# The gate's tanh in its PSUM bank, and the gate's place in the order of a tick

## What is computed

```
logits = x2 @ gate_w.T; the 2 best of 8 experts get softmax weights, the others 0
for each expert e (and the shared one, weight 1):
    a = x2 @ w1[e] + b1[e];  b = x2 @ w3[e] + b3[e]
    y += weight[e] * ((silu(a) * b) @ w2[e] + b2[e])
out = layernorm(x2 + y)
```

## Time and profile before

| | |
|---|---|
| median of 3 runs | 1234.33 us |
| lowest, highest | 1233.46, 1239.96 us |
| span of the profiled execution | 1224.7 us (its own time beside the span isn't shown) |
| TensorE busy | 929.7 us, 76% |
| VectorE busy | 922.6 us, 75% |
| GpSimd busy | 528.2 us, 43% |
| ScalarE busy | 489.6 us, 40% |
| mean granted TensorE clock | 0.798 of full |

### The profile page before, as it was taken

How to read it: one execution, slowest core, us unless ns; L and a number is a source line. 1 busy time by engine, 2 the same in 40 slices (tenths; PEclk the granted TensorE clock), 3 DMA queues, 4 the chain that set the end, 5 groups by cost and what they waited for, 6 DMA issues and landing times.

```text
span 1224.7 us, 13783 instructions
## 1 busy us (share of the span) xinstructions
PE 929.7 (76%) x3960; PEld 700.9 (57%) x3960; DVE 922.6 (75%) x1323; ACT 489.6 (40%) x911; POOL 528.2 (43%) x311
## 2 busy tenths in 40 slices
PE   4845549668689899577689899486789896677996
PEld 2434435256468685165477785165468683554885
DVE  2699996589999966689999965789789965322233
ACT  3534423544246434454345424454245421211442
POOL 1266540453457740533367730544257741001553
PEclk9855558778669999678679899678579997665999
DMA  5100101201023211101023211201023212000331
GB/s 193 36 35 35 52 1 35 70 35 61 18 70 121 77 45 54 70 35 61 18 78 127 73 36 55 85 18 61 18 72 119 86 35 91 21 1 9 117 109 42
DMA packets 38254, 72.61 MB, mean 59 GB/s; under 512 B 3871, under 2 KB 12712, under 8 KB 38174
## 3 DMA queue, kind: packets, MB, share of 16 engines
q1 hardware_dynamic: 38174, 71.65, 17.8%
HBM read 65.14 MB, written 2.30 MB: 55 GB/s over the span
## 4 chain that ended last, share of the span: by engine, by line
PE 45%; DVE 23%; issue 20%; POOL 6%; ACT 3%; DVEq 1%; POOLq 0%; DMA 0%; ACTq 0%; SPq 0%
PE ps L862 11%; DVE hs L1051 7%; PE ps L939 7%; PE ps L718 6%; PE ps L797 5%; POOL dbu L531 4%; DVE yacc L1103 4%; PE ps L836 3%; PE ps L791 2%; PE ps L825 2%; DVE work L1219 2%; PE ps L881 2%; PE ps L776 2%; DVE xn L1014 1%; POOL work L563 1%
## 5 line engine op out<-in xcount | busy, mean ns | idle before, releaser
L531 POOL TENSOR_TENSOR dbu<-v,bbc 128x1024 f32<-128x1024 f32 x128 | 308.9, 2418 | 257.3 <-DVE hs L1051 136.3
L1051 DVE TENSOR_TENSOR_SCAN hs<-ps,carry,dbu 128x512 f32<-128x512 f32 x256 | 313.3, 1266 | 10.1 <-ACT ps L627 8.2
L627 ACT ACTIVATE ps<-delta,neg_a 128x512 f32<-128x512 f32 x256 | 175.7, 692 | 300.5 <-DVE hs L1051 300.4
L718 PE MATMUL ps<-ident,hs 128*128 128x128 f32 x1024 | 189.1, 344 | 116.5 <-DVE yacc L1103 99.5
L718 PEld LDWEIGHTS ps<-ident,hs 128*128 128x128 f32 x1024 | 157.0, 180 | 150.0 <-DVE hs L1051 72.4
L1103 DVE SCALAR_TENSOR_TENSOR yacc<-ps,ctok,yacc 128x512 f32<-128x512 f32 x240 | 167.3, 737 | 1.2 <-PE ps L718 1.0
L555 POOL TENSOR_TENSOR w_lo<-w13s,w_hi 128x512 fp32r<-128x512 f32 x72 | 94.5, 1313 | 145.1 <-ACT w_hi L693 145.1
L939 PE MATMUL ps<-w2s,work 128*128 128x256 f32 x576 | 140.4, 388 | 0.3
L939 PEld LDWEIGHTS ps<-w2s,work 128*128 128x128 f32 x576 | 109.0, 196 | 15.9 <-DVE work L1225 1.5
L1219 DVE SCALAR_TENSOR_TENSOR work<-work 128x512 f32<-128x512 f32 x72 | 82.3, 1143 | 46.5 <-POOL work L563 45.6
L862 PE MATMUL ps<-x_hi,w_hi 128*128 128x512 f32 x288 | 107.9, 457 | 9.4 <-DVE work L1225 9.2
(11 more groups left out here) (159 smaller groups left out, 1243.0 us busy)
## 6 DMA issues: line engine op xcount, KB each, us to landing
w13s<-in_w SPq DMA_DIRECT2D x72, 256.0 KB, 2.9
bbc<-brow_dram SPq DMA_DIRECT2D x32, 512.0 KB, 4.0
w2s<-in_w SPq DMA_DIRECT2D x36, 256.0 KB, 2.7
cbc<-comb_dram SPq DMA_DIRECT2D x32, 256.0 KB, 3.5
work<-work SPq DMA_DIRECT2D x16, 256.0 KB, 2.3
xn<-in_x SPq DMA_DIRECT2D x5, 512.0 KB, 5.3
xt<-in_x SPq DMA_DIRECT2D x4, 512.0 KB, 3.6
rope<-in_rope_q SPq DMA_DIRECT2D x4, 512.0 KB, 4.2
```

What stands on the lines that cost most here:

```text
L531: pool.tensor_tensor(dbu[:, i % DRING, :, :], v[:, 2 * h:2 * h + 2, :], bbc[:, n // 2 % 2, n % 2, :].rearrange("p (o t) -> p o t", o=1) .t ...
L627: act.activation(ps[:, unit % 2, :], delta[:, q, :], ACT.Exp, scale=neg_a[:, q * NS + m:q * NS + m + 1]).then_inc(da_done.sem, 1)
L718: last = pe.transpose(ps[:, bank, t * P:(t + 1) * P], src(t), ident[:, :])
L1051: dve.tensor_tensor_scan(hs[:, m % 2, q, 0:TC], ps[:, unit % 2, :], dbu[:, n % DRING, q % 2, :], carry[:, m, q:q + 1], ALU.mult, ALU.add). ...
```

## The change

The tanh no longer writes `th` in SBUF but overwrites the bank from which it reads, and the product `gm` reads it there. So the bank is busy for longer: the next gate may only start when the product is done, where before it could when the tanh was. The tanh waits for `ga`, which reads the same bank. To this come moves in the order of a tick: the gate's matmuls go from the early to the late part (behind the up matmuls, the scan's transposes and, in the first ticks, the combine transposes and the bias rows, ahead of the down product); `gate_halves` goes from mid to late, behind the scan's exponentials and ahead of the copy of the combine weights; the product `gm` goes from late to mid, ahead of the scans. The exponentials `el` stay where they were. `hh`, the weight split, `gac` and the DMA issues keep their places.

```
-        th = work[:, 0:1024].rearrange("p (a t) -> p a t", a=2)
...
 ScalarE, second
                 if part == "mid":
-                    gate_halves(j, t)
+                    if t == T_TOP:
+                        act.wait_ge(*ls_done.at(j, 1))
+                        act.activation(el[:, :, :], ls[:, :, :], ACT.Exp).then_inc(el_done.sem, 1)
                     return
                 if part == "late":
+                    gate_halves(j, t)
...
             def gate_halves(j, t):
-                if t == T_TOP:
-                    act.wait_ge(*ls_done.at(j, 1))
-                    act.activation(el[:, :, :], ls[:, :, :], ACT.Exp).then_inc(el_done.sem, 1)
...
                     act.activation(ga[:, ib, :], ps[:, 4, :], ACT.Identity, scale=0.5, bias=bias
                                    ).then_inc(ga_done.sem, 1)
-                    act.activation(th[:, ib, :], ps[:, 4, :], ACT.Tanh, scale=0.5, bias=bias
+                    act.wait_ge(*ga_done.at(j, c + 1))
+                    act.activation(ps[:, 4, :], ps[:, 4, :], ACT.Tanh, scale=0.5, bias=bias
                                    ).then_inc(th_done.sem, 1)
...
 TensorE, second_early
                 c = t - T_EXP
-                if 0 <= c < 2 * ALL:
-                    e, ib = divmod(c, 2)
-                    pe.wait_ge(*lo_done.at(j, c + 1))
-                    pe.wait_ge(*th_done.at(j, c))
-                    gate_rows(j, c, 0, a_ps)
                 if 0 <= c - 1 < 2 * ALL:
                     pe.wait_ge(*hh_done.at(j, c - 1))
                     gate_rows(j, c - 1, 1, b_ps)
...
 TensorE, second_late, ahead of the down product
+                c = t - T_EXP
+                if 0 <= c < 2 * ALL:
+                    pe.wait_ge(*lo_done.at(j, c + 1))
+                    pe.wait_ge(*gm_done.at(j, c))
+                    gate_rows(j, c, 0, a_ps)
...
 VectorE: gated_rows(j, t) is called at the end of second_mid, up_rows(j, t) in second_late
+            def gated_rows(j, t):
                 c = t - T_EXP - 1
                 if 0 <= c < 2 * ALL:
                     ib = c % 2
...
-                    dve.scalar_tensor_tensor(out=gm[:, ib, :], in0=th[:, ib, :], scalar=1.0,
+                    dve.scalar_tensor_tensor(out=gm[:, ib, :], in0=ps[:, 4, :], scalar=1.0,
                                              in1=(gac if c >= 2 else ga)[:, ib, :],
                                              op0=ALU.add, op1=ALU.mult).then_inc(gm_done.sem, 1)
+
+            def up_rows(j, t):
+                c = t - T_EXP - 1
+                if 0 <= c < 2 * ALL:
+                    ib = c % 2
                     dve.wait_ge(*gm_done.at(j, c + 1))
                     dve.wait_ge(*b_ps.at(j, c + 1))
```

More of the change, by code:

```diff
@@ L1171, in second_mid @@
                                           ).then_inc(x2lo_done.sem, 1)
+                gated_rows(j, t)
             def relu_rows(j, half):
@@ L1209, in second_late @@
                     combine_weights(j)
+                up_rows(j, t)
+                if t == T_OUT:
+                    for tile in range(NT):
+                        dve.wait_ge(*o_ps.at(j, 2 * ALL))
+                        dve.tensor_tensor(xa[:, tile, :], ps[:, 6 + tile // 2, tile % 2 * DM:(tile % 2 + 1) * DM],
+                                          x2[:, tile, :], ALU.add).then_inc(xo_done.sem, 1)
+                    for tile in range(NT):
+                        row_stats(j, "xo", xa, tile, xo_done)
+                    deviations(j, "xo")
+                    normalise(j, "xo", xa, xa, fin_done)
+            def gated_rows(j, t):
                 c = t - T_EXP - 1
@@ L1226, in second_late @@
                                              in1=gm[:, ib, :], op0=ALU.add, op1=ALU.mult).then_inc(hh_done.sem, 1)
[L1227 to L1235, removed]
             def wide(a):
```

## The result

| | before | after |
|---|---|---|
| median | 1233.89 us (4 runs, 1231.65 to 1239.96) | 1373.76 us (4 runs, 1370.64 to 1380.93) |
| span of the profiled execution | 1224.7 us | 1368.7 us |
| mean granted clock | 0.798 | 0.795 |

The ratio on record is 1.1216, 95% interval 1.1156 to 1.1276. The two medians of the table give 1.113 and the two spans 1.118, so the changed kernel is 11 to 12% slower. In this and all later comparisons the ratio leaves out executions that were over 1.5% longer than the kernel's fastest, while medians and ranges keep them. The forecast was 1394 us, with 1360 to 1430 as its range.

What follows compares the result with a forecast made beforehand. Beside scans TensorE and VectorE were taken as full; the new order closes a loop over four engines. Span 1224.7 + 100.5 (three chunks) + 41.5 (last chunk) + 18 (clock) = 1384.7, plus 9.6 to the median: 1394 us, range 1360 to 1430.

Steps and rivals of the forecast that it cites:

- The loop: Beside scans: second exponential, ga, th, w_hi, w_lo, gac, gm, back to the scans; 8.54 us a tick against 6.5.
- The small steps: Links of the tick beside scans: exponential to ga 0.70, gac to gm 1.38, gm to scans 0.70 us.
- The turn after the scans: Behind the scans and in the last chunk, gm to gate and round to gm through TensorE: 7.24 us.
- Extras: Next chunk's four squares on ScalarE, 1.6 us, and four normalisations on VectorE, about 1.0 beyond its wait.
- The stretched product: VectorE's L1219, one operand now in PSUM: 1.143 to 0.75 us, 28 us less busy time over 72 instances.
- tanh in place: ScalarE's tanh writing PSUM: 0.69 us; waiting for ga, it starts 0.75 after ga's start.
- The last two ticks: End of each chunk's experts, no weights to split, ga straight to gac: 4.7 us each, 9.4 in all.
- The clock term: Gate at low clock, 1.17 us more in 31 ticks without scans: between 0 and 36 us, taken as 18.
- the step from the span to the median of the runs: Median of the runs lies 9.6 us above the profiled span, added to 1384.7 for the forecast.
- the stretches ahead of and behind them: Chunks with scans: late gate(0) before the loop, +4.7 us; from scan pair 13 to the last hh, +3.7.
- The rivals: VectorE freed, 2 in 100; only the gate's own loop closes, 3 (milder form 6); the clock takes over, 9.
- The freed VectorE: Nothing takes the shortened product's place, ticks bound by TensorE or VectorE: 28 us gained, 1206 us; 2 in 100.

Runs made afterwards that it cites:

- number 1: Changed kernel with GpSimd issuing the weighted gate gac ahead of the weight split w_lo: 1235.96 us, ratio 1.0097.
- number 5: Kernel before, old storage and order, with only GpSimd's weighted gate gac moved ahead of w_lo: 1223.59 us, ratio 0.9917.
- 6: Changed kernel with gac ahead of w_lo on GpSimd, gate(0) early and the combine weights' copy ahead of ga(0): 1223.35 us, ratio 0.9919.
- number 11: Kernel before with one edit, the four normalising operations of xn on ScalarE instead of VectorE: 1204.52 us, ratio 0.9802.
- number 3: Changed kernel's order with th back in SBUF and the gate waiting for the tanh only: 1368.87 us, ratio 1.1168.
- number 7: Changed kernel with gac ahead of w_lo, early gate(0), combine copy ahead of ga(0), and ga between the two exponentials: 1223.29 us, ratio 0.9923.

## Why the prediction was right, and where it was off

- **The loop** is right in every link, and number 1 shows it: take the weight split out of it, and of 12.2% more time 1.0% is left (interval 0.5 to 1.5).
- **Its size**, 8.54 us, was 0.2 to 0.3 too much: typical ticks take 8.2 to 8.35. The small steps (ga after the exponential, product after the weighted gate, scans after the product) were each put 0.07 to 0.09 too high. The turn after the scans was 7.04 to 7.11 at full clock, not 7.24. From scan pair 2 to 13 it is 92.8 us in each chunk, where 96.5 were summed.
- **Extras.** The squares cost what was said: one tick of 9.9 us, 1.6 above the others. The normalisations were put at 1.0 and cost next to nothing in the three chunks with experts, where GpSimd stood idle beside them (four in 1.13 us, against 4.5 before): the group fell from 1142 ns to 640.
- **The stretched product** fell to 0.69, 0.06 under the guess; 72 x (1.143 - 0.691) = 32.5 us of VectorE's time and not 28. The sentence that no gain of it can be seen holds.
- **tanh in place** took 0.66 and the start of the tanh came 0.71 to 0.72 after that of ga, against 0.75.
- **The last two ticks** failed: 9.4 was said, and 12.6, 10.9, 10.9 and 12.1 were measured in the four chunks (790.80 to 801.68 in the second, 1342.98 to 1355.06 in the last; the first and the last had part of them at the low clock). The sum had followed the ga loop alone. With gate(17) behind up(16) and behind the down product, TensorE's own queue is longer than that loop, so TensorE sets the last turn: it is busy for all of it, 6.3 us in the two chunks at full clock.
- **The clock term** is the one that was mis-sized most: it was put at 18 us, and the low clock cost some 5. That is 13 of the 20 us that the forecast is too high. Windows of the changed kernel's last chunk:

```profile
1270.00:1278.00 8.00, 6.37 (x20) 4.83 (x20) 1.44 (x2) 1.89 (x3) 2.58 (x3) 0.79 0.26 60
1278.00:1286.00 8.00, 4.74 (x20) 3.69 (x21) 2.22 (x4) 1.89 (x3) 2.51 (x2) 1.00 0.34 99
1286.00:1293.00 7.00, 4.74 (x20) 3.69 (x20) 1.36 (x2) 1.89 (x3) 2.50 (x2) 1.00 0.26 76
```

TensorE has a pause of 2.4 us in each turn at full clock, and the clock is full in two of the three windows. From the second to the sixteenth product are 14 turns; ten of them have a granted clock of 1.00 throughout and four a mean of 0.76 to 0.79. Together they took 101.45 us; at 7.11 each, the usual turn at full clock, that would be 99.5. So the low clock cost at most 2 us there, and about 1.2 in the last two ticks, where the last turn but one took 5.89 at a granted clock of 0.52 and 4.6 in the two chunks at full clock. Of the five ticks behind the scans in each of three chunks, only the last two of the first chunk were touched (0.74 and 0.94), for 1.7 us; the others ran at 1.00. The reasoning went from one row, a pause after which the clock fell, to every pause of such a length, and it took half of the bound for want of a reason. The Trainium skill (TensorE: Matmul & The Clock Gate, "HAM oscillation — how this bites in real kernels") describes a kernel that pays for the low clock in every round; taken over to this loop, the term would have been 36, by the prediction's estimate. The trace disagrees for this loop, whose pauses are shorter: here most rounds run at full clock. That the length of the pauses is the reason no run shows.
- **The rest, and some luck.** 4.5 us are the step from the span to the median of the runs: 9.6 was taken over from the kernel before, and it is 5.1 here (1373.76 less 1368.7). The last 3 us are what is left of larger errors that cancel: the 11 ticks of the loop were put 3.7 us too high in each of three chunks, 11 in all, and the stretches ahead of and behind them and the last chunk 8 us too low together. The mechanism was right; that its sum without the clock came out within 3 us is in part luck.
- **The rivals.** None took place. The freed VectorE did not come out faster even when the loop was shortened: numbers 5 and 6 have the same time, though the product takes 948 ns in the one and 691 in the other.

Where number 11's gain of 24 us (0.0198 x 1232) lies: in the tick that holds the normalisations. Beside the experts that tick falls from 11.65 to 7.24 us (669.11 to 680.76 before, 674.44 to 681.68 in number 11), 13 us in three chunks. In the first body, where a mixer runs alone, it falls from 8.74 to 3.66, 5 us more; there too `dbu` runs on GpSimd beside them (the kernel before):

```profile
155.40 6.99 POOL L531 TENSOR_TENSOR dbu<-v,bbc 128x1024 f32<-128x1024 f32 x3
...
157.94 5.13 DVE L1014 TENSOR_SCALAR xn<-xn,rms 128x256 f32<-128x256 f32 x4
```

That is 18 us, and the two profiled spans differ by 17.8 (1224.7 and 1206.9). The stretches between the chunks' experts differ by 6 to 11 us in either direction and nearly cancel, so the agreement is closer than it had to be, and the step from 18 to 24 stays open.

## What to carry to other kernels

When an operation moves within a tick, write down for each in-order queue what now stands ahead of what, and close the loops: sum starts to starts around each, and compare with the tick. A cheap operation issued ahead of an urgent one (the weight split, needed a tick later, ahead of the weighted gate, needed now) can cost more than any single instruction does. Before paying with a bank and a new wait to shorten a stretched instruction, look whether the stretch is on the path at all, and which other instruction beside the same engine is: here it was a normalisation of 20 instances, and moving that to an engine with air gave 2.0% (number 11), with the swap on GpSimd 2.5 to 2.9%. And when a wait is taken away, look where it went: in number 5 it moved to the next instruction of the same queue.

## What the runs showed of the hardware

- A VectorE product with two SBUF operands that starts 0.07 to 0.09 us after GpSimd's `dbu` takes 2.81 to 2.86 us (30 instances in number 3), and 0.69 alone; with one operand in PSUM it takes 0.69 beside the same `dbu`.
- A VectorE tensor_scalar, which has a single tensor operand in SBUF, is held too: four of 128x256 took 1.13 us with GpSimd idle and 5.24 us beside it. That wasn't expected of a form with one tensor input. The Trainium skill (SBUF — State Buffer, "Who interferes with whom") says it of this operation: it can enter a mode that takes both ports, and then contends with GpSimd. The durations agree; the mode itself isn't seen in a trace. The prediction had told the rule for one SBUF input without this exception. The same four on ScalarE take 1.7 us beside GpSimd's work and in the first body (491 to 508 ns each in four kernels).
- Even a tensor_scalar of 128x4 is held: `ms` took 142 to 159 ns in the changed kernel, and 1.98 us in number 7 beside `dbu` (670.20, `dbu` from 669.77 to 672.15).
- ScalarE's tanh from a PSUM bank to the same bank takes 0.66 us; the one to SBUF took 0.68.
